# Attention scores: one maximum over two PSUM banks, negated maxima cast by ScalarE, value products five steps behind

## What is computed

```python
Q, K = _apply_rope(proj(W_q), ...), _apply_rope(proj(W_k), ...)   # B=4, 16 heads, S=1024, 8
V = proj(W_v)
scores = jnp.einsum('bhnd,bhmd->bhnm', Q, K) / jnp.sqrt(jnp.float32(D_K))
scores = jnp.where(causal[None, None], scores, -jnp.inf)
attn = jax.nn.softmax(scores, axis=-1)
head = jnp.einsum('bhnm,bhmd->bhnd', attn, V)
...
x = x + s * g          # first layer
x = x + s * g          # second layer
```

## Time and profile before

| what | us |
|---|---|
| median of 3 runs | 1015.14 |
| lowest and highest run | 1014.59, 1017.11 |
| span of the profiled execution | 1008.0 |
| attention: first maximum to last cast of maxima | 117.9 to 501.3 |
| one period (one group of four heads) in the steady stretch | 23.85 |

### The profile page before, as it was taken

One profiled execution on the slowest core, in us unless ns is written; L12 is line 12 of the kernel. 1 busy time (PEld: TensorE's weight loads), 2 busy tenths in 40 slices (PEclk: granted clock), 3 DMA queues, 4 the chain that ended last, 5 costly groups with the idle time before them and its releaser, 6 DMA issues. The chain is left out here.

```text
span 1008.0 us, 25094 instructions
## 1 busy us (share of the span) xinstructions
PE 874.2 (87%) x9373; PEld 464.7 (46%) x9374; DVE 816.2 (81%) x1699; ACT 725.7 (72%) x1493; POOL 289.1 (29%) x331
## 2 busy tenths in 40 slices
PE   4999899899999999999898898778999999979960
PEld 3666543334333333333344666533444444458850
DVE  6665499899999999999923766589999999928895
ACT  2666408788888888888784454478999999948851
POOL 4865311111111000000003656500344443005560
PEclk9999859999999999999999888768999999989995
DMA  5579851644445353330004899695354643546637
GB/s 167 223 267 331 280 133 42 205 101 105 110 98 125 89 123 84 68 69 14 13 24 127 277 317 301 226 241 101 67 118 94 114 89 54 136 142 189 206 119 252
DMA packets 121560, 147.20 MB, mean 146 GB/s; under 512 B 19213, under 2 KB 81242, under 8 KB 120800
## 3 DMA queue, kind: packets, MB, share of 16 engines
q1 hardware_dynamic: 116064, 133.74, 48.0%
q0 software_dynamic: 5376, 11.85, 4.1%
HBM read 77.63 MB, written 69.54 MB: 146 GB/s over the span
## 5 line engine op out<-in xcount | busy, mean ns | idle before, releaser
L854 ACT ACTIVATE probsB<-psB 128x512 f32<-128x512 f32 (+2 forms) x640 | 310.0, 566 | 87.1 <-PE psB L928 61.5
L766 DVE TENSOR_REDUCE mxB<-psB 128x1 f32<-128x512 f32 (+2 forms) x448 | 256.9, 642 | 11.1 <-PE psB L892 8.3
L921 PE MATMUL psB<-q_groups,k_groups 64*128 64x512 bf16 (+3 forms) x768 | 205.8, 330 | 16.6 <-DVE mxB L766 8.3
L892 PE MATMUL psB<-k_groups,q_groups 64*128 64x512 bf16 (+3 forms) x768 | 217.0, 344 | 2.8 <-PEq L293 1.7
L959 PE MATMUL psB<-probsB,vB 128*32 128x512 f32 (+3 forms) x1536 | 164.5, 500 | 0.7 <-ACT probsB L854 0.5
L1725 ACT ACTIVATE psD<-psD 128x896 f32<-128x896 f32 (+2 forms) x192 | 153.4, 799 | 12.9 <-PE psD L1779 12.7
L921 PEld LDWEIGHTS psB<-q_groups,k_groups 64*128 64x128 bf16 x768 | 67.5, 94 | 161.2 <-ACT probsB L854 140.3
L1656 DVE TENSOR_REDUCE sumsD<-psD 128x1 f32<-128x128 f32 (+3 forms) x256 | 113.2, 481 | 11.8 <-PE psD L1802 9.4
L899 PE MATMUL psB<-hideB,chooseB 64*128 64x128 bf16 (+1 forms) x1024 | 115.1, 210 | 0.0
L1779 PE MATMUL psD<-k_groups,q_groups 64*128 64x512 bf16 (+3 forms) x384 | 104.4, 343 | 12.3 <-ACT psD L1725 5.6
L766 DVE TENSOR_REDUCE mx2B<-psB 128x1 f32<-128x384 f32 (+2 forms) x192 | 104.4, 594 | 8.5 <-PE psB L899 6.9
(11 more groups left out here) (227 smaller groups left out, 1504.5 us busy)
## 6 DMA issues: line engine op xcount, KB each, us to landing
v<-vaugA SPq DMA_DIRECT2D x4, 2048.0 KB, 8.9
vB<-v SPq DMA_DIRECT2D x16, 512.0 KB
q_groups<-q SPq DMA_DIRECT2D x32, 200.0 KB
k_groups<-k SPq DMA_DIRECT2D x32, 200.0 KB
q_groups<-q SPq DMA_DIRECT2D x32, 192.0 KB
k_groups<-k SPq DMA_DIRECT2D x32, 192.0 KB
back<-emptyB POOLq DMA_DIRECT2D x16, 256.0 KB, 3.8
o<-outB SPq DMA_DIRECT2D x128, 32.0 KB, 1.8
```

The costliest lines, as they stand in the source:

```text
L766: nc.vector.tensor_reduce(dst, src, AX.X, ALU.max).then_inc(max_read, 1)
L854: nc.scalar.activation(probs[:, n % DEEP, 0:w], st[n % BANKS][:, 0:w], ACT.Exp, scale=DH ** -0.5).then_inc(exp_done, 1)
L892: ins = nc.tensor.matmul(bank[:, to:to + w], q[half[r], s, hq // 2, t * P:t * P + P], k[half[r], s, hq // 2, HALF * c:HALF * c + w], start ...
L921: ins = nc.tensor.matmul(bank[:, to:to + w], k[half[r], s, hq // 2, jt * P:jt * P + P], q[half[r], s, hq // 2, i0:i0 + w], start=True, sto ...
```

## The change

Three things are edited in `attention`.

- The maximum ring is read two banks at a time (`SLOT` = 2). `order` holds no turns any more, so it has 640 units; VectorE runs 320 reductions, one for each pair of neighbouring units, which have the same tile and width. It starts when both units of the pair are written. The two heads of a pair go to the two banks by their parity. TensorE waits for a pair's read at even n only, for that of the pair two back.
- The turn goes to a bank of the second scores' ring. A new list `st_order` numbers steps and turns together, and ScalarE casts the turned maxima (`keep_negated`) and raises `exp_done`. SP's wait ahead of `place` is for that. VectorE's cast is gone; its one reciprocal in mid-stream moves to the first pair after the turn.
- The values' products keep LAG = 5, and `due` is as it was; their waits are renumbered by `st_place`.

```diff
--- before.py
+++ after.py
@@ -611,6 +611,7 @@
     last_step = [max(n for n, (j, _) in enumerate(steps) if j == jj) for jj in range(SLOTS_B)]
     AHEAD, DELAY = 16, 4
     RING, BANKS = 4, 3
+    SLOT = 2
     LAG, DEEP = 5, 16
 
     def stream(x):
@@ -620,8 +621,16 @@
         return [u for u in after if u[0] < NQ]
 
     prologue = [(0, g) for g in range(AHEAD)] + stream(-1)
-    order = prologue + [u for x in range(NQ) for u in stream(x)]
+    sequence = prologue + [u for x in range(NQ) for u in stream(x)]
+    order = [u for u in sequence if u[1] is not None]
     place_of = {u: n for n, u in enumerate(order)}
+
+    st_order = [(0, None)]
+    for x in range(NQ):
+        turned_at = next((e for e, u in enumerate(stream(x)) if u[1] is None), None)
+        for e in range(UNITS):
+            st_order += [(x + 1, None)] * (e == turned_at) + [(x, e)]
+    st_place = {u: n for n, u in enumerate(st_order)}
 
     def offset(heads, hq, w):
 
@@ -634,7 +643,7 @@
 
     with Space(nc) as m:
         ps = m.psum("psB")
-        mxb = [ps[:, i, :] for i in range(RING)]
+        mxb = ps[:, 0:RING, :]
         st = [ps[:, RING + i, :] for i in range(BANKS)]
         pv = ps[:, 7, :]
         ident, g2 = second.ident, second.sems
@@ -704,7 +713,7 @@
                 load(0)
                 for x in range(1, QUADS):
                     load(x)
-                sp.wait_ge(max_read, place_of[0, None] + 1)
+                sp.wait_ge(exp_done, st_place[0, None] + 1)
                 place(0)
                 for x in range(NQ):
                     if x == 1:
@@ -715,7 +724,7 @@
                         load_dens(x // QUADS - 1)
                     store(x, 0)
                     if x + 1 < NQ:
-                        sp.wait_ge(max_read, place_of[x + 1, None] + 1)
+                        sp.wait_ge(exp_done, st_place[x + 1, None] + 1)
                         place(x + 1)
                         if x == SCALED - 1:
                             store_rden(0)
@@ -742,30 +751,26 @@
                     dve.wait_ge(g2["den_loaded"], 16 * (b + 1))
                     nc.vector.reciprocal(second.rden[:, b, :], second.den[:, b, :]).then_inc(g2["rden_ready"], 1)
 
-                for n, (x, g) in enumerate(order):
-                    if n == AHEAD:
+                for m in range(len(order) // SLOT):
+                    x, g = order[SLOT * m]
+                    if SLOT * m == AHEAD:
                         nc.vector.memset(empty[:, :, 0:D + 1], 0.0).then_inc(emptied, 1)
                         nc.vector.memset(empty[:, :, D + 1], float(2 * N)).then_inc(emptied, 1)
                     par = x % 2
-                    if (x, g) == (SCALED, None):
+                    if (x, g) == (SCALED + 1, DELAY):
                         reciprocals(0)
-                    dve.wait_ge(max_done, n + 1)
-                    if g is None:
-                        if x >= 2:
-                            dve.wait_ge(neg_placed[par], PLACED * (x // 2))
-                        nc.vector.tensor_copy(neg[:, par, :], mxb[n % RING][0:64, 0:P]).then_inc(max_read, 1)
-                        continue
+                    dve.wait_ge(max_done, SLOT * (m + 1))
                     heads, t, c = units[g]
                     w = max_width(t, c)
                     table, col = (mx, t) if c == 0 else (mx2, t - 4)
+                    both = mxb[:, SLOT * m % RING:SLOT * m % RING + SLOT, :]
                     if len(heads) == 1:
-                        dst, src = table[:, par, heads[0] % 2, heads[0] // 2, col:col + 1], mxb[n % RING][:, 0:w]
+                        dst, src = table[:, par, :, heads[0] // 2, col], both[:, :, 0:w]
                     else:
-                        dst = table[:, par, heads[0] % 2, :, col]
-                        src = mxb[n % RING][:, 0:2 * w].rearrange("p (a w) -> p a w", w=w)
+                        dst, src = table[:, par, :, :, col], both[:, :, 0:2 * w].rearrange("p r (a w) -> p r a w", w=w)
                     nc.vector.tensor_reduce(dst, src, AX.X, ALU.max).then_inc(max_read, 1)
-                    if g == UNITS - 1:
-                        dve.wait_ge(max_read, n + 1)
+                    if g + SLOT == UNITS:
+                        dve.wait_ge(max_read, m + 1)
                         nc.vector.tensor_tensor(mx[:, par, :, :, 4:8], mx[:, par, :, :, 4:8], mx2[:, par, :, :, :],
                                                 ALU.max).then_inc(combined, 1)
 
@@ -840,18 +845,28 @@
                         act.wait_ge(out_stored[c], STORED * x)
                     nc.scalar.copy(out[:, c, :], pv).then_inc(out_kept, 1)
 
+                def keep_negated(x):
+                    at = st_place[x, None]
+                    if x >= 2:
+                        act.wait_ge(neg_placed[x % 2], PLACED * (x // 2))
+                    act.wait_ge(st_done, at + 1)
+                    nc.scalar.copy(neg[:, x % 2, :], st[at % BANKS][0:64, 0:P]).then_inc(exp_done, 1)
+
                 act.wait_ge(g2["in_loaded"], 16)
                 nc.scalar.activation(second.gate[:, :, :], second.u[:, :, :], ACT.Silu).then_inc(g2["gated"], 1)
                 act.wait_ge(g2["init"], 2)
                 nc.scalar.activation(second.warm[:, :], second.eps[:, :], ACT.Exp)
+                keep_negated(0)
                 for x in range(NQ):
                     for e, (j, heads) in enumerate(steps):
-                        n = UNITS * x + e
+                        n, at = UNITS * x + e, st_place[x, e]
                         w = slot_width(j) * len(heads)
+                        if st_order[at - 1] == (x + 1, None):
+                            keep_negated(x + 1)
                         if n >= DEEP:
                             act.wait_ge(pv_done, read_up_to(n - DEEP))
-                        act.wait_ge(st_done, n + 1)
-                        nc.scalar.activation(probs[:, n % DEEP, 0:w], st[n % BANKS][:, 0:w], ACT.Exp,
+                        act.wait_ge(st_done, at + 1)
+                        nc.scalar.activation(probs[:, n % DEEP, 0:w], st[at % BANKS][:, 0:w], ACT.Exp,
                                              scale=DH ** -0.5).then_inc(exp_done, 1)
                         if e == last_step[3] + LAG:
                             keep(x, 0)
@@ -867,12 +882,13 @@
             def _(pe):
                 def turn_over(x):
 
-                    n = place_of[x, None]
-                    pe.wait_ge(max_read, n - RING + 1)
+                    n = st_place[x, None]
+                    if n >= BANKS:
+                        pe.wait_ge(exp_done, n - BANKS + 1)
                     pe.wait_ge(split, 4 * (x + 1))
                     pe.wait_ge(loaded, 16)
-                    nc.tensor.transpose(mxb[n % RING][0:64, 0:P], parts[:, x % 2, :, :].rearrange("p a r -> p (a r)"),
-                                        ident[:, :]).then_inc(max_done, 1)
+                    nc.tensor.transpose(st[n % BANKS][0:64, 0:P], parts[:, x % 2, :, :].rearrange("p a r -> p (a r)"),
+                                        ident[:, :]).then_inc(st_done, 1)
 
                 def for_maximum(x, g):
 
@@ -880,11 +896,11 @@
                     s = x % QUADS
                     heads, t, c = units[g]
                     w = max_width(t, c)
-                    if n >= RING:
-                        pe.wait_ge(max_read, n - RING + 1)
+                    if n >= RING and n % SLOT == 0:
+                        pe.wait_ge(max_read, (n - RING) // SLOT + 1)
                     if g == 0 and x >= GROUPS_AHEAD:
                         pe.wait_ge(in_loaded[s], LOADS * (x // QUADS + 1))
-                    bank = mxb[n % RING]
+                    bank = mxb[:, n // SLOT * SLOT % RING + heads[0] % 2, :]
 
                     def score(i):
                         hq = heads[i]
@@ -910,7 +926,7 @@
                     s = x % QUADS
                     i0 = max(HALF * c, P * jt)
                     w = slot_width(j)
-                    n = UNITS * x + e
+                    n = st_place[x, e]
                     if n >= BANKS:
                         pe.wait_ge(exp_done, n - BANKS + 1)
                     bank = st[n % BANKS]
@@ -948,7 +964,7 @@
                     c, jt = slots[j]
                     s = x % QUADS
                     w = slot_width(j)
-                    pe.wait_ge(exp_done, UNITS * x + last_step[j] + 1)
+                    pe.wait_ge(exp_done, st_place[x, last_step[j]] + 1)
                     if x < GROUPS_AHEAD and j == 0:
                         pe.wait_ge(in_loaded[s], LOADS)
                     if jt == 0 and x + c:
@@ -967,7 +983,7 @@
 
                 def output_projection():
                     pe.wait_ge(g2["const"], 16 * 7)
-                    pe.wait_ge(max_read, len(order))
+                    pe.wait_ge(max_read, len(order) // SLOT)
                     for t in range(NT):
                         if t % 4 == 0:
                             pe.wait_ge(g2["head_ready"], t // 4 + 1)
```

(2 more changed lines are left out.)

## The result

The changed kernel takes **1071.47 us** (median of 4 runs, 1069.0 to 1073.87); beside it the kernel before took 1014.87 us (4 runs, 1010.55 to 1017.11). The ratio is **1.058**, with a 95% interval from 1.0546 to 1.0612: slower by 56.6 us. The forecast was 1061, with a range of 1040 to 1076.

The account below looks back on a forecast made before the run. VectorE was taken as busiest (22.63 of 23.85 us a period), TensorE nearly level. Groups 0 to 13 +42, group 14 +1.9, lead-in +2 took the 1008.0 us span to 1053.9; with 7.1 to median time, 1061 us, range 1040 to 1076.

Parts of the forecast that it names:

- The walk: One steady period of four heads, each start the latest of engine free, bank free and pair full: 27.0 us.
- (1) The merged read: VectorE's reductions: one read of two banks saves one fixed part of two, 1.3 us a group; 512 pair 1.13 us.
- Rival D: Two-bank reads on VectorE pay the fixed part twice, so nothing is saved: +0.6 us a group, 1070 us; chance 0.07.
- (2) The cast: Turned maxima's cast moves to ScalarE: 0.24 us less on VectorE, 0.18 to 0.27 on ScalarE, covered, costed at nothing.
- (3) The period: Four single maximum banks become two pairs: steady period 23.85 to 26.85 us, 3.0 us more a group.
- the pieces overstate today's period: Correction to the walked period: 21.5 + 2.5 exceeds 23.85 by 0.1, so 26.85 us taken instead of 27.0.
- The bound given for a handover: Error allowed at handovers: 0.1 us either way over about nine loops, 0.9 us a group, +-13 us in all.
- (4) Lead-in and group 14: Maxima before any exponential, at half clock: +2 us; group 14, with maxima beside it for 24 steps: +1.9 us.
- A: Rival: pairs cost nothing, handovers hide and VectorE's 1.5 us a group is gained; 990 us; chance 0.08.
- TensorE's own 21.5 us: TensorE's own work in a 23.85 us period, said to leave under 2.4 us of gain; argument against rival A.
- B: Rival: it balances, VectorE's idle time grows by just the 1.5 us it saves; 1015 us; chance 0.03.
- C: Rival: TensorE's clock falls too, a tenth of the period at half clock adding 30 us; 1090 us; chance 0.06.

Follow-up runs that it names:

- Experiment 3: Changed kernel, but each pair is read by two single reductions, both only after the pair is full; 1084.1 us, ratio 1.0703.
- experiment 5: Changed kernel with value products that fell after an even step put one step later, between the pairs; 1031.44 us, ratio 1.0163.
- experiment 1: Kernel before with only the cast moved to ScalarE and the turned maxima in the score ring; 1011.9 us, ratio 0.9979.
- experiment 4: Changed kernel with TensorE's wait for VectorE's read written ahead of its wait for the exponential; 1061.91 us, ratio 1.0476.
- experiment 7: Kernel before, four single banks, with only the value products moved one step later as in experiment 5; 1021.56 us, ratio 1.0041.

## Why the prediction was right or wrong

**What bounds, and the mechanism: right.** The forecast had it that ten products in the middle of pairs would keep VectorE from reading, and that TensorE would wait in return. Experiment 3 shows the first (the wait for the full pair costs 3.86 us of a net 4.00), experiment 5 the second half of the argument (3.1 us go when the products move). For steps 20 to 24 it had VectorE idle 0.95 and TensorE waiting 1.03 and 0.88; the rows have 0.96, 0.98 and 0.80. The walk named steps 0, 4, 12, 16, 20, 24, 32, 34 and the turn as those where TensorE waits; in the trace it waits at just these, and at step 28 behind the turn.

**(1) The merged read: right.** By shape, the reductions of two full banks in the attention of the changed kernel (count, then busy time and mean ns of one):

```profile
L771 DVE TENSOR_REDUCE mxB<-psB 128x2 f32<-128x1024 f32 x160 | 188.5, 1221 | 37.7 <-PE psB L908 29.7 <-PE psB L915 8.0
...
L853 ACT CAST negB<-psB 64x128 bf16<-64x128 f32 x16 | 4.2, 260 | 21.4 <-PE psB L890 21.4
```

One lasts 1.22 us, forecast 1.21. Back to back their pitch is (2.36 - 1.22) = 1.14, forecast 1.13, where two single ones take 1.195. Rival D, a fixed part paid twice, is out. The Trainium skill ("VectorE: DVE Perf Modes", the errata section) gives a read of PSUM a fixed part of 120 cycles at 0.96 GHz, 0.125 us; the pitches here again show about half of it, so that merging saves 0.06 us a pair and not 0.125.

**(2) The cast: right.** It lasts 0.260 us on ScalarE, inside 0.18 to 0.27, and experiment 1 shows that it costs nothing.

**(3) The period: right in kind, short by 1.0 us of 4.0.** The step that failed is a price: "a bank is taken again 0.05 after its reader ends". That was read where the reader is an exponential, whose wait the weight load carries. Where the reader is VectorE, TensorE started 0.10 to 0.15 us after it (0.147 in 70 of the 80 cases from 200 to 480 us): seen above as 302.47 to 302.63. Swapping the waits brings it to 0.06 in 51 of 72 cases and gives back 0.61 us a period, so it was the order of the waits and not the engine. Where that price nearly holds, in experiment 4, the walk's 27.0 stands against 27.24 measured. The remaining 0.39 us is this 0.24, by which the walk fell short, and the 0.15 taken off it because "the pieces overstate today's period": that correction went the wrong way. In the counting of the forecast (20.7 us of work by pitch) VectorE is idle 7.1 us a period where 6.3 was forecast. The bound given for a handover, 0.1 us over about nine loops, held (0.61 of 0.9 us), but with the other two parts the error of a period, 1.0 us, is above it. The time lies in the range, 4.5 us below its upper end, since those bounds were added up with others that were hardly needed (lead-in, cast).

**(4) Lead-in and group 14.** +1.5 for +2, +2.8 for +1.9: small, and with opposite signs. In the lead-in VectorE is busy 28.81 of 31.60 us, so it doesn't keep the pace, as the walk had it.

**The sum.** Terms forecast: 42 + 1.9 + 2 = 45.9. Measured: 53.7 + 2.8 + 1.5 = 58.0. Of the difference of 12.1, groups 0 to 13 make 11.7. What was said of "7.1 us between span and median time" was a misreading that cost nothing: where both are on record, the time of an execution is its span and 1.8 us, so the profiled execution of before, with its span of 1008.0, was one of the short ones, and the other 5.3 us are the spread between executions.

**The rivals.** A (the pairs cost nothing) fell: VectorE is idle ahead of eleven of twenty reads. It wouldn't have held without the pairs' cost either: in experiment 5, with the products out of the way, its 1.5 us don't show. The reason given against it, TensorE's own 21.5 us, is half of why; the other is that no step of the kernel before waited for VectorE. B fell with it: by the same counting VectorE's idle time grew by 5.5 us a period, not by 1.5. C fell: the clock is 1.00 in the steady stretch, with waits of up to 1 us on TensorE.

**What stays open.** Of the 0.9 us left in experiment 5, 0.40 is the later place of the products (experiment 7). The pairs' 0.51 are waits for reads, of which 0.20 is the order of the waits; how the rest would shrink with more pairs is not known, since all eight banks are in use and a ring of three pairs was not tried. Why the walk is 0.24 us short of experiment 4 was not taken apart.

## What to carry to other kernels

Merging two reads saves a fixed part, which the trace prices (0.06 us a pair here), and makes the reader wait for the later of two writers: look at what the writer does between the two. With a ring of only two such units, a long instruction between the halves made first the reader and then the writer stand idle. The engine with the highest busy share need not be the one that is waited for: here VectorE was busy 95% of the time and no step waited for it, so work taken off it was worth nothing. Look for the waits that end on its instructions, by their ends and not by the names in the profile, before saving work on it. And take each handover's price from a row with the same two engines and the same order of waits.

## What the runs showed of the hardware

Where TensorE has two waits ahead of a step, the order of the two counts. In the records of the changed kernel the wait for VectorE's read, written second in the code, is an instruction of its own, lasting 51 ns, ahead of the weight load, which carries the wait for the exponential. A step then starts 0.10 to 0.15 us after the read ends; with the wait for the read written first, and so carried by the weight load, it starts 0.06 us after it in most cases (0.08 to 0.10 in the rest). Writing the wait that ends last ahead of the other in the code was worth 0.61 us a period; the two kernels stand at 1.0579 and 1.0476 of the kernel before, with intervals that don't touch.

A row's releaser can be an engine long done when two waits stand ahead of one instruction: 0.98 us were put down to ScalarE that were VectorE's, as the ends of the instructions above show. The waits of TensorE's weight loads from 200 to 480 us (us in total, times, longest), in the changed kernel and then in experiment 4, say the same:

```profile
PEld psB L937 <- ACT probsB L869: 117.9, 151, 1.5
```

```profile
PEld psB L937 <- ACT probsB L869: 49.0, 61, 0.8
PEld psB L937 <- DVE mxB L771: 47.6, 62, 1.4
...
PEld psB L937 <- DVE mx2B L771: 18.9, 30, 0.9
```

With the order swapped and nothing else changed, 68.9 us leave ScalarE's name and 66.5 stand under VectorE's. In the kernel before, where the exponential is the late one and its wait is on the weight load already, nothing suggests a gain from a swap; it was not run.
